# Attention scores of a 16-head block: three fp32r products of high and low parts in place of one native fp32 product

## The reference

```
h = rmsnorm(x, ln1_w)
q = (h @ wq).reshape(b, s, 16, 128)
k = (h @ wk).reshape(b, s, 16, 128)
v = (h @ wv).reshape(b, s, 16, 128)
scores = einsum('bqhd,bkhd->bhqk', q, k) / sqrt(128)
scores = where(causal, scores, -1e9)
attn = softmax(scores)
ao = einsum('bhqk,bkhd->bqhd', attn, v).reshape(b, s, 2048) @ wo
x = x + ao
```

## Time and profile before

| | |
|---|---|
| Median of 3 runs | 819.42 us (817.55 to 819.58) |
| The profiled execution | 822.67 us |
| Its span, first to last instruction | 820.9 us |
| TensorE matmul busy | 761.7 us, 93% of the span |
| VectorE, ScalarE, GpSimd busy | 430.3, 352.7, 231.1 us |
| Native fp32 matmuls of L1374, share of the chain that ended last | 7% |
| The 16-head attention, in the span | from 338.6 to about 581 us |

### The profile page before, as it was taken

The page is one execution under the profiler, slowest core; times in us unless marked ns, Lnnn a source line. Parts: engine busy times, 40 slices in busy tenths (PEclk is TensorE's granted clock), DMA queues, the critical chain, the costliest instruction groups (busy, mean ns, idle before and its releaser), DMA issues.

```text
span 820.9 us, 13560 instructions
## 1 busy us (share of the span) xinstructions
PE 761.7 (93%) x4626; PEld 621.6 (76%) x4627; DVE 430.3 (52%) x831; ACT 352.7 (43%) x852; POOL 231.1 (28%) x284
## 2 busy tenths in 40 slices
PE   7998899999849985999999999999898999999996
PEld 5887755666537863898898898898686888888885
DVE  6688262111446876345445435436545566656564
ACT  3887302222137874445445455455542233333332
POOL 5110040000355425221321321310423334343430
PEclk9999789999968998999999999999989999999999
DMA  8960031111100002101100110000113334343421
GB/s 318 420 232 2 1 103 46 45 46 37 53 19 2 2 2 76 41 20 34 45 26 32 34 36 32 25 14 1 58 39 91 98 109 118 105 122 101 130 74 51
DMA packets 25670, 58.29 MB, mean 71 GB/s; under 512 B 3600, under 2 KB 14480, under 8 KB 24352
## 3 DMA queue, kind: packets, MB, share of 16 engines
q1 hardware_dynamic: 24864, 55.68, 21.0%
q0 software_dynamic: 768, 2.10, 0.8%
HBM read 51.67 MB, written 6.09 MB: 70 GB/s over the span
## 4 chain that ended last, share of the span: by engine, by line
PE 81%; ACT 6%; DVE 4%; DMA 3%; POOL 2%; issue 2%; POOLq 0%; SPq 0%; PEldq 0%; ACTq 0%; PEld 0%; DVEq 0%
PE PS L329 15%; PE PS L331 15%; PE PS L330 15%; PE PS L1374 7%; PE PS L1099 6%; PE PS L1114 3%; PE PS L441 3%; PE PS L432 2%; PE PS L399 2%; PE PS L405 2%; PE PS L1380 2%; ACT x_probT L523 1%; PE PS L387 1%; ACT x_prob L552 1%; PE PS L454 1%
## 5 line engine op out<-in xcount | busy, mean ns | idle before, releaser
L329 PE MATMUL PS<-tTh,wh 128*128 128x512 f32 x200 | 79.9, 399 | 0.0
L889 ACT ACTIVATE hhh<-hh 128x512 fp32r<-128x512 f32 x50 | 31.6, 632 | 112.2 <-DVE hh L915 100.6
L330 PE MATMUL PS<-tTl,wh 128*128 128x512 f32 x200 | 79.3, 397 | 0.0
L331 PE MATMUL PS<-tTh,wl 128*128 128x512 f32 x200 | 79.3, 397 | 0.0
L513 DVE TENSOR_TENSOR hhl<-hh,hhh 128x512 fp32r<-128x512 f32 x50 | 52.6, 1052 | 34.9 <-ACT hhh L889 34.9
L1481 ACT ACTIVATE sm<-sm,nmx 128x128 f32<-128x128 f32 x128 | 49.7, 391 | 37.5 <-DVE nmx L1538 37.5
L971 POOL TENSOR_TENSOR wl<-wraw,wh 128x512 fp32r<-128x512 f32 (+1 forms) x50 | 58.2, 1163 | 8.4 <-POOL wh L969 7.9
L513 DVE TENSOR_TENSOR oTl<-PS,oTh 128x512 fp32r<-128x512 f32 x32 | 22.1, 692 | 71.6 <-ACT oTh L1475 71.6
L969 POOL CAST wh<-wraw 128x512 fp32r<-128x512 f32 (+1 forms) x50 | 26.1, 521 | 118.2 <-PE PS L331 113.3
L1577 POOL CAST ah<-araw 128x512 fp32r<-128x512 f32 (+1 forms) x32 | 16.6, 518 | 145.0 <-PE PS L331 143.1
L1099 PE MATMUL PS<-WE,xsT 128*128 x120 | 56.4, 594 | 0.1
(11 more groups left out here) (241 smaller groups left out, 1848.4 us busy)
## 6 DMA issues: line engine op xcount, KB each, us to landing
WE<-moe SPq DMA_DIRECT2D x8, 1536.0 KB, 13.8
wraw<-moe SPq DMA_DIRECT2D x25, 384.0 KB, 3.1
araw<-attn SPq DMA_DIRECT2D x16, 384.0 KB, 3.1
cwb<-cw_d SPq DMA_DIRECT2D x20, 256.0 KB, 3.8
WX<-wx SPq DMA_DIRECT2D x2, 1024.0 KB, 8.5
avraw<-attn_v SPq DMA_DIRECT2D x8, 256.0 KB, 3.1
xs_d<-zeros SPq DMA_DIRECT2D x1, 1920.0 KB, 15.9
xs_s<-xs_d SPq DMA_DIRECT2D x15, 128.0 KB, 2.1
```

The source lines that it names most:

```text
L329: nc.tensor.matmul(out, wh_, xh_, start=first, stop=False, **kw)
L330: nc.tensor.matmul(out, wh_, xl_, start=False, stop=False, **kw)
L331: return nc.tensor.matmul(out, wl_, xh_, start=False, stop=last, **kw)
L889: nc.scalar.activation(hhh[half][:, :], hh[half][:, :], ACT.Copy).then_inc(s.hi_done, 1)
```

## The change

Queries and keys are kept as a high and a low part each (fp32r), in place of one fp32 tensor. ScalarE's copy of the queries now writes the high part; VectorE takes the low part out of the same bank of PSUM (`queries_lo`). VectorE's copy of the keys writes the high part, and a second VectorE instruction takes the low part (in `keys`). The scores of a block are one call of `three`: three fp32r matmuls with 128 columns, in place of one native fp32 product. A new semaphore `scores_lo` counts the low parts, four per head, and TensorE waits on it before the scores and before each step that reuses a bank from which queries or keys were read. The probabilities by values stay as they were.

```diff
-        qT_ = [sb(f"aqT{i}", [P, T], where=g) for i in range(2)]
-        kT_ = [sb(f"akT{i}", [P, T], where=g) for i in range(2)]
+        qTh = [sb(f"aqTh{i}", [P, T], F32R, g) for i in range(2)]
+        qTl = [sb(f"aqTl{i}", [P, T], F32R, g) for i in range(2)]
+        kTh = [sb(f"akTh{i}", [P, T], F32R, g) for i in range(2)]
+        kTl = [sb(f"akTl{i}", [P, T], F32R, g) for i in range(2)]
...
+            def scores(par, half, si):
+
+                for t in range(4):
+                    a0 = half * HALF + t * S
+                    m = three(pe, PS[:, si % 4, t * S:(t + 1) * S], qTh[par][:, a0:a0 + S], qTl[par][:, a0:a0 + S],
+                              kTh[par][:, a0:a0 + S], kTl[par][:, a0:a0 + S], True, True)
+                m.then_inc(ring_done, 1)
...
-                pairs(qT_[par], kT_[par], 0, si)
+                pe.wait_ge(scores_lo, 4 * h + 3)
+                scores(par, 0, si)
                 pe.wait_ge(aw_split, 4 * h + 6)
                 proj(h + 1, n, 0, 0, si + 1)
                 pe.wait_ge(ring_dve, d if first else d - 1)
-                pairs(qT_[par], kT_[par], 1, si + 2)
+                pe.wait_ge(scores_lo, 4 * h + 4)
+                scores(par, 1, si + 2)
...
                 proj(h + 1, n, 1, 0, si + 4)
-                pe.wait_ge(ring_act, a + 1)
+                pe.wait_ge(scores_lo, 4 * h + 5)
                 proj(h + 1, n, 1, 1, si + 5)
                 pe.wait_ge(ring_dve, d + 2)
                 turn(h, 0, si + 6)
-                pe.wait_ge(ring_act, a + 2)
+                pe.wait_ge(scores_lo, 4 * h + 6)
                 turn(h, 1, si + 7)
                 if pair is not None:
                     pe.wait_ge(av_split, 2 * pair + 2)
                     for u in range(2):
-                        pe.wait_ge(ring_dve, d + 3 + u)
+                        pe.wait_ge(scores_lo, 4 * h + 7 + u)
                         values(2 * par + u, si + 8 + u)
...
-                pairs(qT_[par], kT_[par], 0, si)
-                pairs(qT_[par], kT_[par], 1, si + 1)
+                pe.wait_ge(scores_lo, 4 * h + 4)
+                scores(par, 0, si)
+                scores(par, 1, si + 1)
...
-                        copy(qT_[n], half, r + 1 + 2 * half, si + 1 + 2 * half, ring_act)
+                        copy(qTh[n], half, r + 1 + 2 * half, si + 1 + 2 * half, ring_act)
...
-            def keys(dst, half, r, si):
+            def keys(par, half, r, si, d):
                 dve.wait_ge(ring_done, r + 1)
-                v.tensor_copy(dst[:, half * HALF:(half + 1) * HALF], PS[:, si % 4, :]).then_inc(ring_dve, 1)
+                cols = slice(half * HALF, (half + 1) * HALF)
+                v.tensor_copy(kTh[par][:, cols], PS[:, si % 4, :]).then_inc(ring_dve, 1)
+                dve.wait_ge(ring_dve, d + 1)
+                split_lo(kTl[par][:, cols], PS[:, si % 4, :], kTh[par][:, cols]).then_inc(scores_lo, 1)
+
+            def queries_lo(par, half, a, si):
+                dve.wait_ge(ring_act, a + 1)
+                cols = slice(half * HALF, (half + 1) * HALF)
+                split_lo(qTl[par][:, cols], PS[:, si % 4, :], qTh[par][:, cols]).then_inc(scores_lo, 1)
...
                 for half in range(2):
                     mask(h, half, r + step * half, si + step * half, d + half)
+                if not last:
+                    for half in range(2):
+                        queries_lo(n, half, PRE_RA + PER_R * h + half, si + 1 + 2 * half)
                 for half in range(2):
                     norm(h, half)
```

More of the change, by code:

```diff
@@ L305, in build @@
             sem(k) for k in ("aw_split", "ring_done", "ring_act", "ring_dve", "ahi_done"))
+        scores_lo = sem("scores_lo")
         masked, aexp_done, norm_done, wo_done = (sem(k) for k in ("masked", "aexp_done", "norm_done", "wo_done"))
@@ L1423, in head @@
                     if pair is None:
-                        pe.wait_ge(ring_dve, d + 3 + half)
+                        pe.wait_ge(scores_lo, 4 * h + 7 + half)
                     pairs(v4[:, place, :], pT, half, si + (8 if pair is None else 10) + half)
@@ L1460, in attn_pe @@
             for k in range(4):
-                pe.wait_ge((ring_act, ring_dve)[k // 2], k % 2 + 1)
+                pe.wait_ge(scores_lo, k + 1)
                 values(k, 4 + k)
@@ L1506, in attn_act @@
             for half in range(2):
-                copy(qT_[0], half, half, half, ring_act)
+                copy(qTh[0], half, half, half, ring_act)
             for k in range(4):
@@ L1557, in head @@
                     for half in range(2):
-                        keys(kT_[n], half, r + 4 + half, si + 4 + half)
+                        keys(n, half, r + 4 + half, si + 4 + half, d + 2 + half)
                 for half in range(2):
@@ L1562, in attn_dve @@
             for half in range(2):
-                keys(kT_[0], half, 2 + half, 2 + half)
+                queries_lo(0, half, half, half)
+            for half in range(2):
+                keys(0, half, 2 + half, 2 + half, half)
             head(0, 0)
```

## The result

The changed kernel takes 841.74 us (median of 4, 839.19 to 845.42) against 819.43 before: a ratio of 1.028, 95% interval 1.025 to 1.031, or +22.3 us. The forecast was 835.2, the range 829 to 843. The direction and the range held; the size fell 6.5 us short, at the price that rival C had.

A forecast was written before the change was run, and what follows sets the result against it. TensorE's own stream was taken to bound the attention. Scores 15.0, last head 0.1 and VectorE waits 0.7 sum to +15.8 us, giving 835.2 us on the median of 819.42; range 829 to 843.

The forecast's parts named there:

- rival C: VectorE's chain to the first values slips by 0.5 us a head and becomes the bound: +7, 842 us; chance 0.07.
- The product: TensorE's scores: each 128-column fp32r product costs its weight load, 0.112 to 0.120 us, taken as 0.116.
- rivals A and B: Score products: A, load hides, only passes count, 813.5 to 817.2, chance 0.11; B, each costs 0.223, 873, chance 0.07.
- The term of 15.0: Longer scores on TensorE's stream in heads 0 to 14: 30 halves at +0.50 us, +15.0 us.
- the last head: There TensorE waits for the softmax, so only the later start of the mask counts: +0.14 us.
- The VectorE chain: VectorE's low parts, from half 1's scores to the first values: 0.05 us late in 14 heads, +0.7 us.
- the first values are 0.02 late: Key low part ready at e+7.48, TensorE there at e+7.46; e is the end of half 1's scores.
- The length of the scores drops out of this: The first values' lateness behind VectorE's chain, counted from the end of half 1's scores, doesn't depend on the scores' length.
- the signs that were set: A head's period of 16.5 to 16.7 us for the forecast; above 17 with distances as forecast for rival C.
- The forecast's own bounds, 833 to 838: Whole time: from 0.112 a product without waits (833) to 0.120 with 2 us of waits (838).
- the prologue and the loads: Before the first scores, four low parts (2.8 us) cost nothing; weight splitting and loads follow TensorE, no DMA added.
- rival D: TensorE's granted clock falls to half for 6.8 us in each head's scores: +51, 886 us; chance 0.03.

The follow-up runs named there:

- e5: e1 with only the first 64 of the 128 columns of keys streamed in each product: 836.59 us (one run).
- e6: e1 with only 64 columns of queries loaded as weights and all 128 columns of keys streamed: 816.33 us (one run).
- e7: e3 with the high and low parts of queries and keys in bf16 in place of fp32r: 815.82 us, ratio 0.996 to the kernel before.
- e1: The changed kernel with three fp32r products of high parts only, no low parts on VectorE and the waits of before: 830.63 us.
- e4: The changed kernel with GpSimd's second weight split of a head held back until the transposes of half 0 are done: 833.43 us.
- e3: The changed kernel with the low part of query half 1 taken behind the two normalisations on VectorE, not ahead of them: 833.62 us.
- e2: The changed kernel with one native fp32 product of the high parts for the scores; low parts and all new waits stay: 830.67 us.

## Why the prediction came out as it did

**The product: right.** The step that took the weight load as the limit, from the router's 16 columns and from equal load times, was right in its mechanism (e5, e6, e7), and rivals A and B fell on it. Of its ends, 0.112 and 0.120, the lower is the true one (0.111); I took 0.116. The term of 15.0 measured 13.2: e1's 13.5 less 0.3 of the last head. The fixed part that fp32r shows at 256 and 512 columns isn't added to the load: at 128 columns 0.111 is all.

**The VectorE chain: right in its links, mis-sized by ten.** I gave it 0.7 us and it cost 8.0 (after less e1). The step that failed is "the first values are 0.02 late", twice over. First, it took the second normalisation at 0.69 as in the earlier trace rows, where GpSimd had hardly begun:

```profile
389.96 0.69 DVE L1545 TENSOR_TENSOR sm<-sm,rsum 128x512 f32<-128x512 f32 x1
```
```profile
390.58 0.40 POOL L1577 CAST ah<-araw 128x256 fp32r<-128x256 f32 x1 [11.83 <-PE PS L331]
```

By the same reckoning that normalisation would run from e+5.47 to e+6.16, and GpSimd's split starts when the output projection ends, which is also on TensorE's clock; I had the durations but never set GpSimd's rows beside them. That is 0.33 of each head's 0.39, 5.1 us over 13 heads with 0.06 of other lateness, and 0.4 in head 14. The 0.06 is what the prediction itself had (0.05), and e4's period, 16.50 against e1's 16.44, shows it alone. Second, it counted head 0 as one of 14 like the others. Head 0 has no output projection, so TensorE reaches the transposes 2.7 us earlier, where VectorE is no earlier: 16.58 less e1's 13.96 is 2.6 us. e3 took away 6.7 of the 8.0 and e4 the 0.33 a head. "The length of the scores drops out of this" holds only in part: with native scores (e2) the distance from the transposes to the first values is 0.13 us longer still.

**Rival C.** Its mechanism, VectorE's chain slipping, came true beside the forecast's and not in its place, at 8.0 us where it was priced at 7. It had a chance of 0.07 although its text said that the first values had no reserve. A chain with zero slack that passes through 14 heads deserved more. The period, 16.83, lies between the signs that were set: above the forecast's 16.7 and below the 17 that would have named C.

**The range: in part luck.** The sum came to +15.8 and the attention measured +21.5. Two errors pull against each other: products and last head were put 1.6 too high (15.1 against 13.5), VectorE 7.3 too low (0.7 against 8.0). The forecast's own bounds, 833 to 838, missed 841.7; it lies in the range only because that was widened to 843, for a product of up to 0.13, which wasn't needed, and for C's lower half.

**The last head** measured +0.3 (e1: 11.5 us from its first scores to the last output projection, before 11.2) against +0.14; **the prologue and the loads** cost nothing that shows (the first scores start at 339.4 in the changed kernel, at 335.4 in e4 with the same prologue, at 338.6 before), and **rival D** did not come in the changed kernel: its clock is 1.00 throughout the stage.

## What to carry to other kernels

Price a small matmul by its weight load as well as by its passes: with 128 columns of fp32 or fp32r weights, products of 16, 64 and 128 streamed columns all start 0.111 to 0.112 us apart, so three fp32r products with a load each lost to one native product with two. When work is added to an engine that is half idle, write the whole chain to the next reader, for the odd first head too, and look up what GpSimd reads at the new time. An engine that stops for a late operand holds up everything queued behind it: put the instruction with the latest input last.

## What the runs showed of the hardware that was not expected

GpSimd loses more by the overlap than VectorE: its cast of 512 elements took 1.07 us in the changed kernel against 0.61, and its subtraction of 256 took 1.04 against 0.74. These two kinds of instruction, 16 of each, make up its 9.7 us more of busy time.

The first distance in a group of scores is uneven in the profile: 0.15 us in half 0, behind native products (389.63 to 389.78), and 0.06 in half 1, behind fp32r ones:

```profile
392.45 0.22 PE L332 MATMUL PS<-akTh,aqTh 128*128 128x128 f32 x1
392.51 0.27 PE L333 MATMUL PS<-akTl,aqTh 128*128 128x128 f32 x1
```

Neither is a cost or a saving. The period of e1 is 0.89 us above before's, which is what 24 products less 16 native records give at 0.112 each; nothing is left over for a change of kind. Once the load is short, an fp32r product of 128 streamed columns (0.061 in e6) costs nearly what a bf16 one does (0.056 in e7).
